# A fused layer on one core: the first stage's queues reordered, the rounding constant taken off on ScalarE, masked CB in PSUM, chains interleaved

## The chip, the cores and the metric

One core of a Trainium2 chip runs the whole program. The metric is the device time of one execution in microseconds (us). The engines are named as in the profile: PE is TensorE, DVE is VectorE, ACT is ScalarE, POOL is GpSimd, SP issues DMAs. Each has its own queue and works it off in order; semaphores order them against each other. SBUF is the large on-chip memory, PSUM the one that PE writes.

## What is computed

8192 tokens (64 sequences of 128) pass through an embedding, a state-space layer (SSD) and a mixture of experts. All in float32:

```python
scale = jnp.maximum(jnp.max(jnp.abs(weight), axis=-1, keepdims=True) / 127, 1e-8)
h = (jnp.clip(jnp.round(weight / scale), -127, 127) * scale)[input]       # rows of 192

zxbcdt = layernorm(h) @ in_proj_w.T                  # z 384, xBC 384 + 2 * 128, dt 6
dt = softplus(zxbcdt[..., -6:] + dt_bias)
xBC = silu(sum(conv_w[:, k] * xp[:, k:k + L, :] for k in range(4)) + conv_b)
CB = einsum('bcln,bcsn->bcls', C, B)                 # one chunk of 128 a sequence
Y = einsum('bcls,bhcls,bcshp->bclhp', CB, exp(segsum(dt * A)), x * dt) + D * x
y = Y * silu(z);  y = y * rsqrt(mean(y * y) + eps) * norm_w
h = h + sigmoid(gate1) * (y @ out_proj_w.T) + layernorm(h)

h2 = layernorm(h)                                    # route_c, route_u: argmax of two softmaxes of 4
common = expert(route_c)(h2)                         # gelu(x @ W1 + b1) @ W2 + b2, 192 -> 768 -> 192
dropped = rank within route_c (by confidence) >= 2048
out = h + common + dropped * expert(route_u)(h2)
```

## The kernel before

The program has two stages. The first is a software pipeline over 16 groups of four sequences. In turn `t`, `body(t, g1, g2, g3, g4, g5)` works on five groups at once: the embedding and first norm of group `t` and `t + 1`, the projection and convolution of group `t - 1` (`g2`), the SSD of `t - 2` (`g3`), output product, residual and second norm of `t - 3` (`g4`), and the routing of `t - 4` (`g5`). Turns 0 to 17 make the stage. The second stage runs expert units of 256 tokens (gather, two products, scatter), with a search for the capacity threshold beside it; the diff leaves it alone but for the places where it calls functions of the first.

The order of the work within a turn is written out by hand, once for each engine (`body` in each of the blocks `tensor`, `scalar`, `vector`, `gpsimd`). Since queues are worked off in order, a wait holds everything behind it.

The steps that matter, with their lines:

- `project(m)` (PE, L1131): tile m of the projection, 5 of xBC (m < 5), 3 of z. The part over the last 64 channels is issued for two tiles at once in the odd m (L1151), so both become ready then. Only two banks, `mm0` and `mm1`, hold them: `project(m)` waits until tile m - 2 has been read.
- `start(m)` (ACT, L795): first tap and bias out of PSUM into `xbc` (m < 5); z tiles by copy or Silu. `conv(m)` (DVE, L1518): the three other taps, each reading PSUM and `xbc` and waiting for the one before. `silus` (ACT): Silu over all of `xbc`, then over the first z tile.
- `cbx(j)` (PE, L1077): for sequence j, C·B and the transposes of x into the bank `cx`. `seg(j)` (PE, L1057): the differences of running sums into banks `sg0` and `sg1`, which `decays(j)` (ACT, L784) empties by Exp into `dec`. `weights(j)` (DVE, L1533): `cbm` = CB times the causal mask, `xd` = x times dt, and `mix` = min(dec, 1) times `cbm`, six heads of 128. `y(j)` (PE): the product of the two, then `y(j)` (DVE, L1549) adds D·x, and `gate_y(j)` (POOL, L541) multiplies by Silu of z.
- `softplus` (DVE, L1488): ten small operations, each waiting for the one before, that give dt and at the end `drep`; `step_sums` (PE) and `sum_rows` (ACT, L823) turn these into the rows `rows_s` that `seg` of the next turn reads.
- `squares` (ACT), `side` (PE, L1100), `copy_side` (ACT), `side_back` (PE), `side_read` (DVE, L1469): sums of squares, dt and routing values of a group, collected by small products, transposed and read once.
- `quantise(g)` (DVE, L1420) finds the scale of gathered rows; `rounded(g)` (ACT, L773) multiplies and adds 12582912, which rounds; `clip(g)` (DVE, L1431) subtracts that constant and clips, in two passes of 128x768, and takes the statistics. `norm1`, `normed`, `with_rest`, `to_tp`, `from_tp` bring the normed rows to the transposed tiles that `project` reads.
- `residual`, `stats2`, `logits`, `pick`, `places` (DVE), `prefixes` (PE), `list_tokens` (POOL): second residual and norm, routing, running counts `acc` and `more` for each expert, and the lists of tokens. Routing goes in batches of two groups, so that `logits` and `pick` stand in every second turn, `places`, `prefixes` and `list_tokens` in the others.

A `Chain` counts operations of one engine that need each other: `link(ins)` issues one and waits until it has finished; `link.go(ins)` issues only, and `link.join()` waits later.

## Time and profile before

| | us |
|---|---|
| median of 3 runs | 1097.21 (1094.24 to 1099.18) |
| profiled execution | 1107.01 |
| its span, first to last instruction | 1105.2 |
| busy, share of the span: PE | 84% |
| DVE | 61% |
| ACT | 51% |
| POOL | 52% |
| mean granted TensorE clock | 0.925 of 2.4 GHz |

The page gives shares over the whole span; the 40 slices of its second part show which engine is full when. Below that the trace can be asked for windows (busy time by stretch), for groups of instructions by line, and for timelines, in which a bracket names the idle time ahead of an instruction and what ended it. "issue" in it is idle time for which the profile shows no releaser. PEclk is the granted clock as a share of full speed.

### The profile page before, as it was taken

Reading aid. Unit: us, or ns where it says so; the run is one execution under the profiler, and the core shown is the slowest. Engines: PE = TensorE matmul, PEld = TensorE weight load, DVE = VectorE, ACT = ScalarE, POOL = GpSimd, SP = SyncE. Lnnn points to the kernel's source line nnn. Section 1 sums busy time; section 2 is a strip of 40 time slices with the busy share of each in tenths; the row PEclk is TensorE's granted clock in tenths of the full one; section 3 lists DMA queues with packets and bytes.
Section 4 is the critical chain, followed back from the end, with each engine's and each line's share of the span. In section 5 each row is a group of like instructions: output and inputs, shape, how many; then the busy total and the mean of one; then the engine's idle time right before and its main releaser. Section 6 shows DMA issues by size and latency. Waiting matters only on the chain.

```text
span 1105.2 us, 18876 instructions
## 1 busy us (share of the span) xinstructions
PE 931.3 (84%) x5730; PEld 626.5 (57%) x5731; DVE 679.1 (61%) x2089; ACT 564.6 (51%) x1163; POOL 573.0 (52%) x751
## 2 busy tenths in 40 slices
PE   2688899888888889989888597999897977979986
PEld 2233455445554555545546475767675756768874
DVE  3687999898998989889887234777211211112111
ACT  3666886777767877588664224232232221323330
POOL 7332645456465655463434555234556656556543
PEclk9898998999999998899997788999888979889988
DMA  4910011001110111010001122133332111112211
GB/s 101 319 50 2 15 44 45 30 17 45 44 42 6 44 45 45 2 45 30 30 31 60 34 64 66 58 99 111 90 89 54 54 46 49 49 54 73 73 56 29
DMA packets 50179, 61.91 MB, mean 56 GB/s; under 512 B 22668, under 2 KB 41832, under 8 KB 49556
## 3 DMA queue, kind: packets, MB, share of 16 engines
q0 software_dynamic: 16704, 30.54, 9.8%
q1 hardware_dynamic: 28724, 24.91, 7.6%
q10 hardware_dynamic: 4640, 5.13, 1.5%
q8 instruction: 51, 0.84, 0.3%
q14 instruction: 60, 0.49, 0.1%
HBM read 36.22 MB, written 25.92 MB: 56 GB/s over the span
## 4 chain that ended last, share of the span: by engine, by line
PE 40%; DVE 24%; issue 13%; ACT 12%; another core or an unknown queue 5%; POOL 3%; DMA 2%; DVEq 1%; ACTq 0%; POOLq 0%
DVE xbc L1526 9%; PE yb L1304 5%; PE mm L1147 5%; PE cx L1304 5%; PE mm L1282 4%; PE mm L1275 4%; PE mm L1151 3%; PE sg L1275 3%; DVE mix L1546 2%; PE tp L1114 2%; PE sg L1065 2%; ACT rows_s L831 2%; DVE ybuf L1559 2%; DMA xg<-hr_dram,ids 1%
## 5 line engine op out<-in xcount | busy, mean ns | idle before, releaser
L1526 DVE SCALAR_TENSOR_TENSOR xbc<-mm,cw,xbc 128x508 f32<-128x508 f32 (+2 forms) x231 | 168.5, 741 | 27.5 <-ACT xbc L806 19.9
L1147 PE MATMUL mm<-xt_a,win_a 128*128 128x512 f32 x248 | 144.2, 666 | 38.0 <-DVE xbc L1526 28.8
L979 ACT ACTIVATE ht<-mm,b1s 128x256 f32<-128x256 f32 x102 | 44.8, 473 | 256.8 <-PE sg L1275 119.9
L689 POOL DMA_INDIRECT out_dram<-osb,ids_s x80 | 81.9, 1024 | 139.4 <-DVE osb L1900 122.9
L1900 DVE TENSOR_TENSOR osb<-cx,res 128x192 f32<-128x192 f32 x40 | 14.3, 357 | 180.0 <-remote 90.3
L806 ACT ACTIVATE xbc<-mm,cb,cw 128x512 f32<-128x512 f32 x77 | 56.5, 774 | 123.2 <-PE mm L1151 122.2
L549 POOL TENSOR_TENSOR ybuf<-ybuf,zs 128x384 f32<-128x384 f32 x64 | 69.3, 1084 | 73.7 <-DVE ybuf L1559 71.6
L670 POOL DMA_INDIRECT xg<-hr_dram,ids x80 | 80.4, 1005 | 47.6 <-issue 23.8
L1304 PE MATMUL yb<-w2s,ht 128*128 x408 | 85.1, 359 | 10.3 <-issue 10.2
L1304 PE MATMUL cx<-w2s,ht 128*128 x408 | 77.8, 337 | 14.9 <-issue 14.9
L1275 PE MATMUL mm<-fx_a,w1a_t 128*128 128x256 f32 x240 | 82.1, 426 | 9.6 <-issue 5.7
L1304 PEld LDWEIGHTS yb<-w2s,ht 128*128 128x128 f32 x408 | 75.6, 210 | 18.2 <-issue 17.9
L1147 PEld LDWEIGHTS mm<-xt_a,win_a 128*128 128x128 f32 x248 | 39.3, 199 | 76.1 <-DVE xbc L1526 47.2
L1065 PE MATMUL sg<-rows_s,rows_t 32*128 32x384 f32 x256 | 62.8, 568 | 18.9 <-ACT rows_s L831 17.5
L1546 DVE SCALAR_TENSOR_TENSOR mix<-dec,cbm 128x768 f32<-128x768 f32 x64 | 72.0, 1125 | 10.5 <-ACT dec L791 10.5
L608 POOL DMA_INDIRECT list_c<-tok,desti x64 | 64.6, 1010 | 26.2 <-issue 18.1
L1282 PE MATMUL mm<-fx_b,w1b_t 64*128 64x256 f32 x240 | 77.3, 431 | 0.0
L1282 PE MATMUL sg<-fx_b,w1b_t 64*128 64x256 f32 x240 | 77.3, 431 | 0.0
L1304 PEld LDWEIGHTS cx<-w2s,ht 128*128 128x128 f32 x408 | 68.2, 196 | 13.8 <-issue 13.5
L1275 PE MATMUL sg<-fx_a,w1a_t 128*128 128x256 f32 x240 | 74.9, 395 | 0.0
L1151 PE MATMUL mm<-xt_b,win_b 64*128 64x512 f32 x248 | 74.5, 679 | 0.0
L517 POOL DMA_INDIRECT gath<-in_table_dram,gidx x64 | 63.9, 998 | 19.6 <-issue 14.9
(304 smaller groups left out, 2101.1 us busy)
## 6 DMA issues: line engine op xcount, KB each, us to landing
hr_dram<-hr SPq DMA_DIRECT2D x16, 768.0 KB
w2s<-in_w2c_dram SPq DMA_DIRECT2D x4, 576.0 KB
w2s_u<-in_w2u_dram ACTq DMA_DIRECT2D x4, 576.0 KB
list_c<-fill SPq DMA_DIRECT2D x2, 1032.0 KB, 12.4
list_u<-fill SPq DMA_DIRECT2D x2, 1032.0 KB, 18.7
w1a<-in_w1c_dram SPq DMA_DIRECT2D x4, 384.0 KB
w1a_u<-in_w1u_dram ACTq DMA_DIRECT2D x4, 384.0 KB
xg<-hr_dram,ids POOLq DMA_INDIRECT x80
```

The source lines that it names most:

```text
L549: nc.gpsimd.tensor_tensor(ybuf[:, p, :, js], ybuf[:, p, :, js], zs[:, p, :, js], ALU.mult).then_inc(s_y2, 1)
L608: nc.gpsimd.indirect_dma_start(out=list_c[:, :], out_offset=bass.IndirectOffsetOnAxis(ap=desti[:, p, j:j + 1], axis=0), in_=tok[:, GS * fi ...
L670: nc.gpsimd.indirect_dma_start(out=xg[:, v, t, :], out_offset=None, in_=rows, in_offset=bass.IndirectOffsetOnAxis(ap=ids[:, v, t, 0:1], ax ...
L689: nc.gpsimd.indirect_dma_start(out=out_rows, out_offset=bass.IndirectOffsetOnAxis(ap=ids_s[:, v, t, 0:1], axis=0), in_=osb[:, v, t, :], in ...
L1065: last = mmul(bank_[:, 0:HPB * P], rows_t[r:r + ROWS, :], rows_s[r:r + ROWS, j // 2, :, :], start=True, stop=True)
L1147: mmul(tile_bank(g2, m)[:, :], win_a[:, column(m):column(m) + P], xt_a[:, p, :], start=True, stop=False)
L1151: mmul(tile_bank(g2, m - 1 + n)[:, :], win_b[r, c0:c0 + P], xt_b[r, p, :], start=False, stop=True).then_inc(s_mm, 1)
L1275: last = mmul(hid[n][c // 2][:, c % 2 * TL:(c % 2 + 1) * TL], w1a_t[:, v, (3 * n + c) * P:(3 * n + c + 1) * P], fx_a[:, :], start=first, s ...
L1282: last = mmul(hid[n][c // 2][:, c % 2 * TL:(c % 2 + 1) * TL], w1b_t[r, v, c * P:(c + 1) * P], fx_b[r, :], start=first, stop=not first)
L1304: last = mmul(outp[t][:, 0:D], ht[:, v, k, t * P:(t + 1) * P], w2_[:, ds(e * (FC * D) + k * D, D)], start=(k == 0), stop=(k == FC - 1))
L1526: ins = stt(out=dst_[:, :, back:L], in0=src[:, :, 0:L - back], scalar=cw[:, m, TAPS - 1 - back:TAPS - back], in1=dst_[:, :, back:L], op0=A ...
L1546: stt(out=mix[:, j % 2, :, :], in0=dec[:, j % 2, :, :], scalar=1.0, in1=cbm[:, :].unsqueeze(1).broadcast_to([P, HEADS, P]), op0=ALU.min, o ...
```

## The change

Orders first. DVE takes `logits` and `conv(0)` ahead of `weights(0)`; `weights(j)` is cut into `scaled(j)` (mask and x·dt) and `mixed(j)`, which stand apart with other work between; `quantise` goes behind `side_read`. ACT takes `start(0)` ahead of `decays(0)`, `decays(3)`, `with_rest`, `from_tp(0)` ahead of `start(4)`, and the rounding ahead of the Silus. PE takes both first projections ahead of `cbx(0)`, `side` ahead of `y(1)`, `to_tp(0)` ahead of `project(5)`, and `step_sums` last. In `clip` the subtraction goes to ACT as a fifth pass. The masked CB is written back into its PSUM bank, so `cbx(j + 1)` waits for `mix` j. The steps of softplus, of pick and of the second statistics are issued between other operations. The running count lies in the same tile as the one-hots (`oh` has two more rows, used from either end in turn), and one reduction adds it up. The gathers take their index straight from `xids`.

```diff
-STEPS = dict(norm=5, quant=2, clip=3, ...)
+STEPS = dict(norm=5, quant=2, clip=2, ...)
@@ gpsimd
-                nc.gpsimd.tensor_copy(gidx[:, p, :], xids[:, GS * g:GS * (g + 1)]).then_inc(s_idx, 1)
-                pool.wait_ge(s_idx, g + 1)
...
-                        in_offset=bass.IndirectOffsetOnAxis(ap=gidx[:, p, j:j + 1], axis=0)).then_inc(s_gath[p], 16)
+                        in_offset=bass.IndirectOffsetOnAxis(ap=xids[:, GS * g + j:GS * g + j + 1], axis=0)).then_inc(s_gath[p], 16)
@@ scalar, rounded
-                last.then_inc(s_rd, 1)
+                last.then_inc(s_whole, 1)
+                act.wait_ge(s_whole, g + 1)
+                nc.scalar.activation(h0[:, :, :], h0[:, :, :], ACT.Identity, bias=magic[:, 1:2], scale=1.0).then_inc(s_rd, 1)
@@ scalar, order of a turn
+                start(0)
                 decays(0)
-                start(0)
                 start(1)
                 decays(1)
                 normed2()
                 squares()
-
+                exp_logits()
                 start(2)
                 start(3)
                 decays(2)
                 normed()
                 copy_side()
-
-                start(4)
-                exp_steps()
-                start(5)
-                exp_logits()
+                decays(3)
                 with_rest()
                 from_tp(0)
-                decays(3)
-                silus()
+                exp_steps()
+                start(4)
+                start(5)
                 if t + 1 < NG:
                     rounded(t + 1)
+                silu_z()
+                silu_xbc()
                 from_tp(1)
                 start(6)
                 start(7)
@@ tensor, cbx
-                    wait(pe, s_xd, GS * g3 + j)
+                    wait(pe, s_m, GS * g3 + j)
@@ tensor, order of a turn
                 project(0)
+                project(1)
                 cbx(0)
+                prefixes()
                 seg(0)
-                project(1)
                 seg(1)
-                prefixes()
+                project(2)
+                cbx(1)
                 y(0)
-                cbx(1)
-
-                project(2)
+                seg(2)
                 project(3)
-                seg(2)
+                side()
                 y(1)
-                side()
-
+                seg(3)
+                cbx(2)
                 project(4)
-                cbx(2)
+                to_tp(0)
                 side_back()
                 project(5)
                 out_product(0)
-                to_tp(0)
-                seg(3)
+                to_tp(1)
+                cbx(3)
                 y(2)
-
                 project(6)
-                cbx(3)
                 out_product(1)
-                to_tp(1)
-                step_sums()
                 project(7)
                 y(3)
+                step_sums()
@@ vector
-                link(ts(h0[:, :, :], h0[:, :, :], MAGIC, QMAX, ALU.subtract, ALU.min))
-                link(ts(h0[:, :, :], h0[:, :, :], -QMAX, None, ALU.max))
+                link(ts(h0[:, :, :], h0[:, :, :], QMAX, -QMAX, ALU.min, ALU.max))
...
-                        if back < TAPS - 1:
-                            link(ins)
+                            link.go(ins)
+                            beside[back - 1]()
+                            link.join()
...
-                    link(tt(cbm[:, :], cx[:, 0:P], le[:, :], ALU.mult))
+                    link.go(tt(cx[:, 0:P], cx[:, 0:P], le[:, :], ALU.mult))
...
+                def mixed(j):
+                    chains["ssd"].join()
                     dve.wait_ge(s_e, GS * g3 + j + 1)
                     stt(out=mix[:, j % 2, :, :], in0=dec[:, j % 2, :, :], scalar=1.0,
-                        in1=cbm[:, :].unsqueeze(1).broadcast_to([P, HEADS, P]), op0=ALU.min, op1=ALU.mult).then_inc(s_m, 1)
+                        in1=cx[:, 0:P].unsqueeze(1).broadcast_to([P, HEADS, P]), op0=ALU.min, op1=ALU.mult).then_inc(s_m, 1)
...
-                    v.tensor_reduce(more[:, :], oh[:, 0:n5, 0, :].rearrange("p j e -> p e j"), AX.X, ALU.add).then_inc(s_oh, 1)
...
-                    tt(acc[:, :], acc[:, :], more[:, :], ALU.add)
+                    v.tensor_reduce(running(b + 1), with_running(b, n), AX.X, ALU.add)
@@ vector, new order of a turn (all of it)
+                logits(); conv(0); weights(0); conv(1); y(0)
+                scaled(1); places(); mixed(1); conv(2); conv(3)
+                scaled(2); y(1); side_read(); steps_abs(); quantise(t + 1); mixed(2)
+                conv(4, (soft_sum, soft_inverse)); soft_ratio()
+                residual(0, (0,)); soft_square(); residual(0, (1,)); soft_top()
+                scaled(3); soft_term(3); mixed(3); soft_term(2); soft_term(1); soft_term(0); soft_steps()
+                y(2); residual(1); soft_rates(); rows_read()
+                pick((row_moments 0 to 3, row_sums, row_shift))
+                y(3); clip(t + 1)
@@ vector, old order of a turn (all of it)
-                weights(0); conv(0); conv(1); y(0); places()
-                weights(1); conv(2); conv(3); y(1)
-                quantise(t + 1); side_read(); steps_abs(); logits()
-                weights(2); conv(4); residual(0); softplus(); y(2)
-                weights(3); residual(1); pick(); stats2(); y(3); clip(t + 1)
```

(The two orders of DVE's turn are set on fewer lines here than in the code.)

## Rows read from the trace of the kernel before

**Rows 1.** The page: busy tenths of DVE in 40 slices of the span.

```profile
DVE  3687999898998989889887234777211211112111
```

**Rows 2.** Windows: us, busy us (x) PE, PEld, DVE, ACT, POOL, PEclk, DMA.

```profile
127.49:552.86 425.37, 376.32 (x2678) 216.39 (x2676) 385.44 (x1077) 317.39 (x588) 231.31 (x351) 0.97 0.11 33
...
321.63:357.06 35.43, 31.34 (x228) 17.82 (x225) 30.44 (x83) 27.04 (x50) 21.03 (x31) 1.00 0.12 35
357.06:392.59 35.53, 29.88 (x225) 17.54 (x223) 34.07 (x100) 26.36 (x49) 20.87 (x31) 1.00 0.11 35
...
428.77:466.60 37.83, 34.92 (x229) 21.43 (x228) 34.30 (x100) 26.95 (x50) 20.89 (x31) 0.86 0.11 34
...
611.40:1105.20 493.80, 416.64 (x2216) 333.25 (x2214) 157.93 (x641) 137.87 (x372) 258.35 (x264) 0.89 0.23 64
```

**Rows 3.** Timeline of DVE, turn starts: start, us, instruction, [idle before <-releaser].

```profile
340.49 0.26 DVE L1540 TENSOR_TENSOR cbm<-cx,le 128x128 f32<-128x128 f32 x1
...
342.52 0.96 DVE L1546 SCALAR_TENSOR_TENSOR mix<-dec,cbm 128x768 f32<-128x768 f32 x1 [1.18 <-ACT dec L791]
344.29 4.50 DVE L1526 SCALAR_TENSOR_TENSOR xbc<-mm,cw,xbc 128x508 f32<-128x508 f32 x6 [0.81 <-ACT xbc L806]
...
377.66 0.26 DVE L1540 TENSOR_TENSOR cbm<-cx,le 128x128 f32<-128x128 f32 x1
...
411.44 0.26 DVE L1540 TENSOR_TENSOR cbm<-cx,le 128x128 f32<-128x128 f32 x1
```

**Rows 4.** Timeline of DVE: the two clip passes.

```profile
375.01 0.55 DVE L1434 TENSOR_SCALAR h<-h 128x768 f32<-128x768 f32 x1
375.60 0.56 DVE L1435 TENSOR_SCALAR h<-h 128x768 f32<-128x768 f32 x1
```

**Rows 5.** DVE by line, 127.49:552.86: xcount | busy us, mean ns | idle before.

```profile
L1546 DVE SCALAR_TENSOR_TENSOR mix<-dec,cbm 128x768 f32<-128x768 f32 x48 | 54.7, 1139 | 5.0 <-ACT dec L791 5.0
...
L1637 DVE TENSOR_TENSOR acc<-acc,more 128x4 f32<-128x4 f32 x6 | 5.0, 836 | 0.2
```

**Rows 6.** Line 1526, the taps: xcount, ns min/median/max, first and last start.

```profile
L1526 DVE SCALAR_TENSOR_TENSOR xbc<-mm,cw,xbc x231: 732/740/749, 33.5 to 575.4; 128x508 f32<-128x508 f32 x39, 128x500 f32<-128x500 f32 x39, 128x504 f32<-128x504 f32 x38
```

**Rows 7.** Timelines of POOL and DVE: gate product, mix beside it.

```profile
359.71 1.00 POOL L549 TENSOR_TENSOR ybuf<-ybuf,zs 128x384 f32<-128x384 f32 x1
...
360.05 1.48 DVE L1546 SCALAR_TENSOR_TENSOR mix<-dec,cbm 128x768 f32<-128x768 f32 x1
```

**Rows 8.** Timeline of DVE in pick: two that wait, two that don't.

```profile
371.33 0.22 DVE L1613 TENSOR_REDUCE m<-pk 128x16 f32<-128x64 f32 x1
371.59 0.22 DVE L1614 TENSOR_TENSOR oh<-pk,m 128x64 f32<-128x64 f32 x1
...
372.34 0.17 DVE L1618 COPY ohc<-oh 128x32 f32<-128x32 f32 x1
372.42 0.17 DVE L1619 COPY ohu<-oh 128x32 f32<-128x32 f32 x1
```

**Rows 9.** ACT by line, 127:553: start(m) and the rounding passes.

```profile
L806 ACT ACTIVATE xbc<-mm,cb,cw 128x512 f32<-128x512 f32 x60 | 44.0, 774 | 93.8 <-PE mm L1151 92.8 <-issue 1.0
...
L778 ACT ACTIVATE h<-gath,magic,q 128x192 f32<-128x192 f32 x44 | 20.3, 533 | 0.0
```

**Rows 10.** Timeline of ACT: table load ahead of the first decays.

```profile
340.32 1.28 ACT L791 ACT_TABLE_LOAD   x1
```

**Rows 11.** Timeline of PE: gap in side, seg, projection, slow seg.

```profile
320.87 0.88 PE L1114 MATMUL tp<-ybuf,wy 128*32 128x128 f32 x20 [1.00 <-issue]
...
340.36 0.91 PE L1065 MATMUL sg<-rows_s,rows_t 32*128 32x384 f32 x4 [1.19 <-ACT rows_s L831]
...
342.25 1.13 PE L1151 MATMUL mm<-xt_b,win_b 64*128 64x512 f32 x4
...
449.13 1.65 PE L1065 MATMUL sg<-rows_s,rows_t 32*128 32x384 f32 x4
```

**Rows 12.** Timeline of POOL: gate product behind the list transfers.

```profile
345.60 1.00 POOL L549 TENSOR_TENSOR ybuf<-ybuf,zs 128x384 f32<-128x384 f32 x1
```

More of the change, by code:

```diff
@@ L192, in build @@
         ohu = sb("ohu", [P, SEQS, NE])
-        acc, more = sb("acc", [P, NE]), sb("more", [P, NE])
         w1a = sb("w1a", [P, NE * F])
@@ L721, in _ @@
             norm2()
+            route()
             gather_unit(0, 1, 1, 1)
@@ L1194, in prefixes @@
                     wait(pe, s_h1, 2 * cap(t - 3 if t <= LAST_SSD else t - 2))
+                    oh_, acc = picked(b, n)[:, :, 0, :], running(b)
                     if b == BATCHES - 1:
@@ L1516, in softplus, with nothing, conv @@
                     last.then_inc(s_dt, 1)
-                def conv(m):
+                def nothing():
+                    pass
+                def conv(m, beside=(nothing, nothing)):
                     if g2 is None:
@@ L1585, in stats2, with rows_read, row_moments, row_sums @@
                                chains["h1"]).then_inc(s_ve2, 1)
+                    chains["h1"].end()
+                def rows_read():
+                    if g4 is not None:
+                        dve.wait_ge(s_h1, 2 * g4 + 2)
+                        wait(dve, s_xn2, g4)
+                def row_moments(j):
+                    if g4 is not None:
+                        ins = v.bn_stats(st2[:, j, :], hr[:, g4 % 2, j, 0:D])
+                        if j == GS - 1:
+                            chains["h1"].go(ins)
+                def row_sums():
+                    if g4 is None:
+                        return
+                    chains["h1"].join()
+                    for j in range(GS):
+                        last = v.bn_aggr(mv2[:, j, :], st2[:, j, :])
+                    chains["h1"].go(last)
+                def row_shift():
+                    if g4 is None:
+                        return
+                    chains["h1"].join()
+                    ts(var2[:, :], mv2[:, :, 1], LNEPS, None, ALU.add)
+                    ts(minus2[:, :], mv2[:, :, 0], -1.0, None, ALU.mult).then_inc(s_ve2, 1)
                     chains["h1"].end()
@@ L1599, in logits, with pick @@
                     link.end()
-                def pick():
+                def pick(beside=(nothing,) * 6):
                     if b5 is None:
+                        for other in beside:
+                            other()
                         return
```

207 lines of the change are left out of this document (135 added, 72 removed).

## The prediction

> **What bounds the kernel now.** I read the page first. In its 40 slices the Vector engine (DVE) stands at nine tenths in most slices from the third to the twenty-first, and then drops to one or two, while PE stays high to the end: two stages, and the change touches only the first [rows 1]. The windows by stretch give sizes. From 127.49 to 552.86 us, twelve turns of 35.45 us, DVE is busy for 385.44 of 425.37 us, PE for 376.32, ACT for 317.39, POOL for 231.31. After 611.40 come 493.8 us in which DVE is busy for 158: the expert units, which no edit reaches [rows 2].
>
> Third, DVE's timeline. Turns alternate. One with logits and pick (the L turn, 340.49 to 377.66) takes 37.17 us, one with places (the P turn, to 411.44) 33.79: a pair is 70.95. The L turn has 2.0 us of waits at its start: `mix` waits 1.18 for ACT's decays, the first tap 0.81 for ACT's first copy out of PSUM [rows 3]. Three more waits of 0.5 to 0.65 stand in the pair, so DVE works for about 67.2 us of 70.95. DVE sets the pace, PE is close behind: its busy time at full clock is 31.34 and 29.88 us in the two windows of one pair, 30.6 a turn [rows 2].
>
> **The change part by part: DVE.** All sums are for a pair.
>
> The clip pass that subtracts the rounding constant starts 0.59 us ahead of the next one: 2 x 0.59 = 1.2 us removed [rows 4].
>
> `mix`: 48 of them take 1139 ns on average, an undisturbed one 0.96 [rows 3, 5]. The excess comes when POOL runs a tensor operation: its gate product starts at 359.71 and takes 1.00, `mix` starts at 360.05 and takes 1.48 [rows 7]. The masked CB in PSUM leaves `mix` one SBUF tensor. No such `mix` is in this trace. The nearest rows are the taps, one tensor in PSUM and one in SBUF: 231 of them lie between 732 and 749 ns, so POOL never stretched one [rows 6]. Bounds: nothing gained (even 0.06 us lost each, if PSUM reads are dearer) to 0.19 us each. I take 0.19, as the taps are alike in kind: 8 x 0.19 = 1.5.
>
> The running count `acc` plus `more` takes 836 ns for 4 elements, beside the same POOL product, plus 0.12 for `more` [rows 5]. One reduction with one input replaces both, 0.2 us: 0.7 saved.
>
> Interleaved chains: an operation that waits for the one before it starts 0.26 us after it (371.33 to 371.59), one that doesn't starts 0.08 us after it (372.34 to 372.42) [rows 8]. With the larger operand of the chain counted, a hidden wait is worth about 0.12 us. Six in pick (L turn only), six of softplus and two in the last channel's taps each turn, one behind each of the eight CB maskings: 6 + 16 + 8 = 30 waits, 3.6 us; I take 3.2, as some of the filling operations wait themselves. The Trainium skill (VectorE: DVE Perf Modes, The DRAIN you can't avoid) says that eight copies take the same time with a semaphore after each as with one behind the last. By it these 3.2 us would be nothing; these rows disagree for small operations.
>
> DVE's work falls by 1.2 + 1.5 + 0.7 + 3.2 = 6.6 us, from 67.2 to 60.6: 30.3 a turn. That is below PE's 30.6, so what is late next is PE.
>
> **ACT.** It takes the constant off instead: one pass over 128x768. The 192-wide form takes 533 ns, the 512-wide one 774, so 0.75 ns an element: an estimate of 0.97 us, and it must wait for the four passes before it, 0.1 more [rows 9]. ACT goes from 26.4 to 27.5 us a turn, idle before it being mostly the waits for projections (93.8 us over the twelve turns, before copies out of PSUM) [rows 9]. Behind that wait stand both Silus, `from_tp(1)` and the last two z tiles, which release PE's next project(0). Its bounds are 0.8 and 1.3 us. With no cover it costs 1.1 us a turn.
>
> **The order.** I lay the new queues out with these durations (PE: projection pair 3.06 us, seg 0.86 [rows 11]; CB and transposes 0.71, y 0.8, side 2.2, out product 2.0, prefixes 2.1, by the starts on PE's timeline; all of PE's pieces sum to 30.4 a turn, against 30.6 in [rows 2]). Zero is PE's project(0). Project(1) ends at 3.06, ACT's start(0) lets conv(0) begin at 4.05. seg(0) ends at 4.6. Here is a new wait: ACT's table load of 1.28 us stands before the first decay, now behind start(0), and seg(1) needs the banks that decays(0) empties [rows 10]. So seg(1) starts at 6.1, and PE, in order, holds project(2), cbx(1) and y(0) behind it; 1.5 us idle. In P turns prefixes fill it, but then it all comes 1.6 us later. DVE has conv(0) as cover meanwhile, so the 2.0 us at the start of a turn go. Then conv(1) ends at 10.0, project(3) at 12.4, and conv(2) begins at 13.3 after 1.0 us of wait; side ends at 14.6, side_back at 18.6; conv(3) ends at 17.7, project(5) at 20.7. start(4), moved behind `with_rest` and `from_tp(0)`, is on ACT at 20.8. ACT then runs start(5), the rounding with its new pass, the table load, Silu of z and of xBC, from_tp(1), start(6): to 30.4. PE reaches y(3) and the step sums at 30.8, DVE its last clip at 34.85, which is 4.05 of the next turn. All three engines close the turn within 0.5 us of each other: 30.8 us for L, and by the same steps 32.5 for P, 31.7 on average.
>
> The new wait of cbx(j+1) for `mix` j instead of `xd` j costs nothing while a scaled and mixed pair lies two convs ahead of its cbx. In the last turn of the stage (from 592 us) there are no taps: there it puts about 0.9 us in each of two or three places: 1.5 to 2 us lost. Gather's direct index saves POOL 0.5 us a turn, off the path; rounding reached earlier helps the gathers.
>
> Layouts by hand have no gaps. The trace has: PE stands still for 1.00 us within side with nothing to wait for [rows 11], about once a turn. So I add 1.0: 32.7 a turn instead of 35.45. Over twelve turns 33 us; the three outer turns, with DVE less full, 2 each: 6; less 1.5 for the last: 37.5. Clock: at the lower level seg takes 1.65 instead of 0.91 us [rows 11], and the window at 0.86 holds 34.92 us of PE work [rows 2]. Three such stretches lie in the stage; DVE's pace covered most of them, and will no longer. The forecast takes nothing for them beyond the 1.0, nor for small gains in turns 0 and 1.
>
> Against the profiled execution, 1107.0 us of which 1105.2 are span: 1069.5. The median of the runs is 1097.2, 9.8 lower; 3.4% of it is 37.5, so 1059.7; I say 1059.
>
> **Rivals.**
>
> A, bubbles take half of it. PE queue waits in order: if what I count as 1.0 us of gaps and 1.5 at seg(1) is double, because side now stands ahead of y(1), seg(3), cbx(2) and project(4) and itself waits for ACT's squares (which are done at 11.0 against 12.4 needed), a turn takes 34.2. For it: PE and ACT slack of under 1 us everywhere in the layout; in the P turn POOL's gate_y(3) comes after four list transfers [rows 12] and only 0.8 us before squares need it. Against: ACT waits 8 us a turn for projections now, room to slip. Saving 1.25 x 12 + 3: 1097 - 18 = 1079.
>
> B, the Vector engine keeps its work: the chains give nothing (the skill's rule above) and `mix` is as long as now in PSUM. Then only 1.9 of 6.6 go, DVE works 32.65 a turn, about 33.6 with a wait of 1: saving 1.85 x 12 + 5 = 27, 1070. Against it stand [rows 6, 8]. The rule of the skill alone (3.2 of 6.6 gone) would leave DVE 31.9 a turn, 33.2 with its waits, and give about 1065; of B's chance 0.02 is for it.
>
> C, slower: TensorE's clock. DVE hid it before; now PE's work is the turn. In the stretch at 0.86 PE worked 34.92 us in 37.83. With the 2.0 us of waits of the new order such a turn is 36.9. If the whole first stage ran so, it would be 1.45 x 15 = 22 us slower: 1119. It decides from a granted mean of about 0.9 in that stage, 0.97 now. For it: the drops are there, and came in turns whose rows before them look like those of turns without one (the 1.19 us of wait for `rows_s` is in each) [rows 11]. Against: PE gets fuller, not emptier, and in the first stage most windows are at 1.00.
>
> **How the numbers follow.** The forecast, 1059, with its own range 1042 to 1070 (all gaps gone: 31.7 a turn and 49 us saved, 1048, and 6 for the outer turns; `mix` or ACT's pass at the bad end): 0.55. A, 1079: 0.25. B, 1070: 0.10. C, 1119: 0.04. The rest, 0.06, is spread, a third of it slower. The range runs from 1040 to 1086. A measurement of this kernel tells about 0.5% from no change, 5.5 us. Faster by more: 0.88. Within: 0.06. Slower by more: 0.06.
>
> **What would show it.** In the new profile: first stage shorter by about 38 us, the second alike; DVE busy near 30 us a turn and no longer the fullest, PE above it; every `mix` near 0.95 to 1.0 us; the count's reduction near 0.2; small operations 0.1 apart; one ACT pass of about 1 us; PE idle before seg(1), by ACT `dec`, of 1 to 1.5 us; no wait of the first conv on `dec`. Wrong if `mix` still varies with POOL, if ACT's rounding is what releases the clip or project(0) late, if PE waits for ACT's squares in side, or if the granted clock of the first stage falls below 0.9.

## The result, and the profile after

Beside each other, 20 runs each: before 1098.16 us (1091.07 to 1105.71), after 1089.78 us (1080.29 to 1097.51). The ratio is 0.9909, 95% interval 0.9882 to 0.9937: faster by 8.4 us, where 38 were forecast, and outside the range. The profiled execution took 1090.97 us, 1089.2 of them span. The one of before took 1107.01, some 9 above its median, so the two profiles lie 16 us apart where the medians lie 8.4.

The page of after, DVE and the granted clock in 40 slices of the span, and the engines' shares of the chain that ended last; below them the windows (us, busy us (x) PE, PEld, DVE, ACT, POOL, PEclk, DMA) of the first and second stage:

```profile
DVE  3668898979988889788787136787121112112220
...
PEclk9889999999998889888988788999898988989998
...
PE 66%; issue 12%; DVE 8%; ACT 6%; another core or an unknown queue 4%; POOL 2%; DMA 1%; DVEq 1%; POOLq 0%; ACTq 0%
```

```profile
127.00:548.00 421.00, 392.56 (x2685) 225.52 (x2686) 361.36 (x1062) 333.32 (x604) 214.97 (x344) 0.93 0.11 34
598.20:1089.00 490.80, 414.79 (x2219) 328.87 (x2217) 158.00 (x641) 138.66 (x372) 259.33 (x264) 0.91 0.23 65
```

Against [rows 1, 2], DVE has fallen from 385 to 361 us in a window of about twelve turns, and PE has risen from 376 to 393: PE is now the fullest engine, at a granted clock of 0.93 instead of 0.97. The first expert unit starts at 598.2 instead of 610.7. So in these two profiles the first stage is 12.5 us shorter, not 38, and the second nearly alike (491 us for 494). The twelve turns average 34.9 us (418.4 over 12) against a forecast of 32.7. Here and below a turn runs from one masking of sequence 0's CB on DVE to the next.

The pieces on DVE and ACT came as forecast. Timeline of DVE (a masking, xd, `mix`, a tap; the count's reduction) and of ACT (the new pass), and line 1595, the `mix` of that window, with ns min/median/max:

```profile
262.83 0.29 DVE L1584 TENSOR_TENSOR cx<-cx,le 128x128 f32<-128x128 f32 x1
263.02 0.55 DVE L1586 TENSOR_TENSOR xd<-cx,dts 128x384 f32<-128x384 f32 x1
263.49 0.94 DVE L1595 SCALAR_TENSOR_TENSOR mix<-dec,cx 128x768 f32<-128x768 f32 x1
264.35 0.74 DVE L1570 SCALAR_TENSOR_TENSOR xbc<-mm,cw,xbc 128x508 f32<-128x508 f32 x1
...
302.07 0.22 DVE L1735 TENSOR_REDUCE oh<-oh 128x4 f32<-128x36 f32 x1
```

```profile
280.34 0.94 ACT L794 ACTIVATE h<-h,magic 128x768 f32<-128x768 f32 x1
```

```profile
L1595 DVE SCALAR_TENSOR_TENSOR mix<-dec,cx x49: 935/945/955, 128.0 to 546.4; 128x768 f32<-128x768 f32 x49
```

There is no wait between the `xd` at 263.02, the `mix` and the tap: the 2.0 us of [rows 3] are gone. What is new stands on PE. Its timeline in one L turn, ACT's beside it, and windows of 2 us over the same stretch (PEclk is the third number from the end):

```profile
327.99 0.92 PE L1084 MATMUL sg<-rows_s,rows_t 32*128 32x384 f32 x4
330.51 1.65 PE L1084 MATMUL sg<-rows_s,rows_t 32*128 32x384 f32 x4 [1.61 <-ACT dec L805]
332.10 2.08 PE L1166 MATMUL mm<-xt_a,win_a 128*128 128x512 f32 x2
```

```profile
328.20 1.28 ACT L805 ACT_TABLE_LOAD   x1
329.50 0.87 ACT L805 ACTIVATE dec<-sg 128x384 f32<-128x384 f32 x2
```

```profile
328.00:330.00 2.00, 0.91 (x5) 0.29 (x4) 1.93 (x8) 1.97 (x4) 1.38 (x2) 1.00 0.01 2
330.00:332.00 2.00, 1.49 (x4) 0.53 (x4) 1.97 (x5) 1.04 (x2) 1.62 (x2) 0.62 0.03 6
332.00:334.00 2.00, 2.00 (x5) 0.88 (x4) 1.93 (x4) 1.80 (x5) 1.75 (x2) 0.50 0.09 16
334.00:336.00 2.00, 2.00 (x14) 1.67 (x14) 0.51 (x1) 2.00 (x3) 1.75 (x6) 0.50 0.02 4
336.00:338.00 2.00, 2.00 (x13) 1.02 (x10) 1.17 (x5) 0.33 (x2) 1.84 (x5) 0.67 0.00 0
```

seg(1) waits 1.61 us for decays(0), which stand behind the table load, as laid out. But then the granted clock goes from 1.00 to 0.50, that is from 2.4 to 1.2 GHz, and stays there for almost 7 us. seg(1) takes 1.65 us instead of 0.92. Such a stretch stands near the start of all seven turns from 330 us on; most turns before them have none or one of half that length. From 30 to 620 us the time at 1.2 GHz ("low clock" below) sums to 105 us; in the trace of before to 60.

And in P turns side is longer than before. PE's timeline, products of four with nothing to wait for:

```profile
305.40 0.42 PE L1133 MATMUL tp<-ybuf,wy 128*32 128x128 f32 x4 [0.30 <-issue]
306.12 0.43 PE L1133 MATMUL tp<-ybuf,wy 128*32 128x128 f32 x4 [0.30 <-issue]
306.85 0.42 PE L1133 MATMUL tp<-ybuf,wy 128*32 128x128 f32 x3 [0.31 <-issue]
307.58 0.27 PE L1133 MATMUL tp<-ybuf,wy 128*32 128x128 f32 x1 [0.30 <-issue]
308.30 0.28 PE L1133 MATMUL tp<-ybuf,wy 128*32 128x128 f32 x1 [0.45 <-issue]
```

Undisturbed, side takes 2.23 us (in L turns, in both traces). In P turns it took up to 4.4 before and takes 4.9 to 5.8 now (3.3 in the first).

### The profile page after: what moved, and what is told of

Same layout as the page of the kernel before. It is cut to its first block, busy times and chain, and to the rows that moved or that the text cites. A ratio compares the mean times of both kernels' runs of the same rounds, so it can differ in the third digit from the quotient of the medians.

```text
span 1089.2 us, 18793 instructions
## 1 busy us (share of the span) xinstructions
PE 942.1 (86%) x5730; PEld 630.2 (58%) x5731; DVE 643.2 (59%) x2064; ACT 584.1 (54%) x1179; POOL 548.2 (50%) x736
## 4 chain that ended last, share of the span: by engine, by line
PE 66%; issue 12%; DVE 8%; ACT 6%; another core or an unknown queue 4%; POOL 2%; DMA 1%; DVEq 1%; POOLq 0%; ACTq 0%
PE mm L1166 11%; PE mm L1170 6%; PE misc L1181 5%; PE yb L1321 5%; PE sg L1084 5%; PE cx L1321 5%; PE yb L1115 5%; PE mm L1299 4%; PE mm L1292 4%; PE tp L1133 3%; PE sg L1292 3%; PE cx L1105 2%; PE cx L1103 2%; DVE xbc L1570 2%
## 5 line engine op out<-in xcount | busy, mean ns | idle before, releaser
L559 POOL TENSOR_TENSOR ybuf<-ybuf,zs 128x384 f32<-128x384 f32 x64 | 64.2, 1003 | 111.9 <-DVE ybuf L1613 109.9
L1084 PE MATMUL sg<-rows_s,rows_t 32*128 32x384 f32 x256 | 67.9, 608 | 24.9 <-ACT dec L805 22.9
L1321 PEld LDWEIGHTS yb<-w2s,ht 128*128 128x128 f32 x408 | 73.1, 204 | 24.9 <-issue 24.4
L1181 PEld LDWEIGHTS misc<-wo,ybuf 128*128 128x128 f32 x384 | 63.7, 194 | 20.7 <-issue 19.5
L805 ACT ACTIVATE dec<-sg 128x384 f32<-128x384 f32 x128 | 55.7, 490 | 35.5 <-PE sg L1084 34.2
L527 POOL DMA_INDIRECT gath<-in_table_dram,xids x64 | 63.2, 988 | 19.4 <-issue 17.0
L1181 PE MATMUL misc<-wo,ybuf 128*128 128x192 f32 x384 | 71.4, 337 | 1.5 <-DVE sd L1494 1.4
L660 POOL DMA_INDIRECT list_u<-tok,slot_u x64 | 62.9, 982 | 19.5 <-issue 19.5
```

What stands on the lines that cost most here:

```text
L527: nc.gpsimd.indirect_dma_start(out=gath[:, p, j, :], out_offset=None, in_=A["table"][:, :], in_offset=bass.IndirectOffsetOnAxis(ap=xids[:, ...
L559: nc.gpsimd.tensor_tensor(ybuf[:, p, :, js], ybuf[:, p, :, js], zs[:, p, :, js], ALU.mult).then_inc(s_y2, 1)
L1084: last = mmul(bank_[:, 0:HPB * P], rows_t[r:r + ROWS, :], rows_s[r:r + ROWS, j // 2, :, :], start=True, stop=True)
L1181: last = mmul(misc[:, OUTC + j * D:OUTC + (j + 1) * D], ybuf[:, g4 % 2, c, (2 * q + j) * L:(2 * q + j + 1) * L], wo[:, c, :], start=(c == ...
L1321: last = mmul(outp[t][:, 0:D], ht[:, v, k, t * P:(t + 1) * P], w2_[:, ds(e * (FC * D) + k * D, D)], start=(k == 0), stop=(k == FC - 1))
```

## The experiments

All start from the changed kernel unless said. The kernel before took about 1030 us beside some kernels and about 1100 beside others, on the same chips (last section), so all comparisons are by the ratio to the kernel before in the same batch; that level is given with each. Rows with the same level were run together; between rows of different levels a small difference says less than its interval. Only the change and spare_product were run at both levels. "Units" is the start of the first expert unit, and "low" the time at 1.2 GHz from 30 to 620 us, both in the profiled execution (before: 610.7 and 60).

| kernel | level | ratio, 95% interval | units, us | low, us |
|---|---|---|---|---|
| lists_late | 1031 | 0.9965, 0.9938 to 0.9992 | 595.6 | 119 |
| seg_first | 1031 | 0.9816, 0.9777 to 0.9855 | 590.2 | 130 |
| spare_product | 1031 | 0.9651, 0.9620 to 0.9681 | 565.7 | 61 |
| work_only | 1031 | 1.0123, 1.0093 to 1.0153 | 611.2 | 77 |
| the change again | 1099 | 0.9895, 0.9845 to 0.9945 | 595.7 | 99 |
| orders_only | 1099 | 0.9996, 0.9964 to 1.0028 | 610.7 | 109 |
| spare_elsewhere | 1099 | 0.9967, 0.9934 to 1.0000 | 603.3 | 92 |
| seg_first_spare | 1099 | 0.9755, 0.9710 to 0.9800 | 580.9 | 65 |
| spare_again | 1106 | 0.9791, 0.9746 to 0.9836 | 582.6 | 59 |
| spare_lists_late | 1106 | 0.9718, 0.9681 to 0.9756 | 576.8 | 55 |
| linked | 1106 | 1.0035, 1.0008 to 1.0063 | 614.7 | 51 |
| mask_sbuf | 1106 | 0.9584, 0.9550 to 0.9618 | 563.3 | 54 |
| mask_sbuf_no_spare | 1030 | 0.9863, 0.9818 to 0.9908 | 590.3 | 102 |
| seg_first_mask | 1030 | 0.9615, 0.9584 to 0.9647 | 559.2 | 48 |
| clip_on_dve | 1030 | 0.9691, 0.9663 to 0.9719 | 572.0 | 75 |
| lists_end | 1030 | 0.9666, 0.9632 to 0.9699 | 567.6 | 48 |
| seg_first_mask again | 1028 | 0.9609, 0.9575 to 0.9642 | 559.2 | 45 |
| the change once more | 1028 | 0.9852, 0.9821 to 0.9883 | 585.1 | 102 |

### Does PE's wait at seg(1) cost the clock?

In PE's turn, one product that nothing reads, where PE waits (spare_product, spare_again) or later, behind seg(2), where it doesn't (spare_elsewhere):

```
 seg(0)
+mmul(tp[:, :], ident[:, :], xt_a[:, g2 % 2, :], start=True, stop=True)   # spare_product
 seg(1)
 project(2); cbx(1); y(0)
 seg(2)
+mmul(...the same...)                                                      # spare_elsewhere
```

> The changed kernel with one product more in each turn on PE, between seg(0) and seg(1): a 128x512 product into the transposing bank that nothing reads, about 1.0 us, in the place of the wait for decays(0). Theory 3, the low level of the clock in every later turn (6.8 us at 1.2 GHz from the turn's start) comes from the emptiness there: low time in the first stage falls from 105 us to about 60 as before, mean clock of 127 to 548 us from 0.93 to 0.97, and the time by 10 to 20 us to 1070 to 1080, though PE has 16 us of work more. Otherwise: low time as it was, and the time 1090 to 1096.

> As spare_product, with the same unread 128x512 product into tp, but behind seg(2), where TensorE has no idle time, instead of ahead of seg(1). Theory 1 (the product helped since it filled the idle time ahead of seg(1)): low stretches as in the changed kernel, 100 to 120 us; ratio as the changed kernel's or up to 0.3% above it (0.43 us of product a turn). Theory 2 (any more work on TensorE, or the shift of tp, would have done it): as spare_product, ratio 0.965, 61 us of low clock.

> The changed kernel itself, on the same chip as the experiments. Theory 1 (the wait of seg(1) behind the decays brings TensorE's clock down, wherever it runs): granted clock of stage 1 about 0.92 to 0.93, low stretches of 6.8 us in most turns, 100 to 130 us of low clock in all, ratio to the kernel before 0.99 to 1.00 (lists_late, nearly the same kernel, gave 0.9965). Theory 2 (what was lost on the first chip is the gaps of 0.30 us inside side's products, beside the list transfers): without such gaps on this chip the ratio is 0.97 to 0.975, and the low stretches are no more than the 60 us of the kernel before.

> The changed kernel beside it. On the faster chip, where it has not been run: theory 1 (the gaps in side are only on the other chip, the clock is lost on both): side 2.23 in P turns, 100 to 120 us of low clock, ratio 0.990 to 0.998, since lists_late, nearly the same kernel, gave 0.9965 there. Theory 2 (lists_late was itself worse than the changed kernel where there are no gaps): 0.975 to 0.988. On the slower chip: 0.99 as twice before.

The same added work gives 0.9651 (level 1031) and 0.9791 (1106) ahead of seg(1), and 0.9967 behind seg(2); the change itself has 0.9852 (1028), 0.9895 and 0.9909 (about 1099). Windows of spare_product, spare_elsewhere and the change once more; how long the seg products waited in the change and in spare_product (line, x, busy us, mean ns, idle before); and the added product in an L turn, with the seg(1) behind it:

```profile
127.00:548.00 421.00, 408.14 (x2913) 234.37 (x2911) 384.47 (x1158) 352.54 (x635) 222.19 (x351) 0.96 0.11 36
```

```profile
127.00:548.00 421.00, 395.49 (x2704) 227.28 (x2704) 358.38 (x1058) 332.58 (x601) 212.73 (x340) 0.94 0.11 34
```

```profile
127.00:548.00 421.00, 398.82 (x2803) 230.45 (x2803) 370.06 (x1080) 341.07 (x618) 217.25 (x345) 0.92 0.11 34
```

```profile
L1084 PE MATMUL sg<-rows_s,rows_t 32*128 32x384 f32 x196 | 52.5, 614 | 17.6 <-ACT dec L805 17.6
```

```profile
L1084 PE MATMUL sg<-rows_s,rows_t 32*128 32x384 f32 x208 | 51.5, 572 | 6.5 <-ACT dec L805 4.4 <-ACT rows_s L851 2.1
```

```profile
314.07 1.12 PE L1092 MATMUL tp<-xt_a,ident 128*128 128x512 f32 x2
315.75 0.91 PE L1084 MATMUL sg<-rows_s,rows_t 32*128 32x384 f32 x4 [0.55 <-ACT dec L805]
```

The product takes 1.1 us at full clock (the expectation of spare_elsewhere has 0.43, which is too little) and fits into the wait of 1.6. With the idle time filled, the waits of the seg products fall from 17.6 us (in both traces of the change) to 6.5, low clock from 102 to 61 us, and the first expert unit starts at 565.7 instead of 585.1. The same product later leaves 92 us of low clock, against 99 in its batch, and makes the kernel no faster than the change but some 0.7% slower, with intervals that meet. So it is the idle time at that place, not added work or its tile. Each pair below is from two batches of nearly one level: the product is worth 0.020 (0.9852 to 0.9651, 21 us) where side has no gaps, and 0.010 (0.9895 to 0.9791, 11 us, give or take 7 by the two intervals) where it has. At the upper level P turns were to be 33 to 34 us with a ratio of at most 0.978; the later ones are 34.2 to 34.8 at full clock, and the ratio just misses it. The change once more has the ratio of its theory 2 and the low clock and the short side of its theory 1: lists_late was 1.1% worse than the change, so the "0.9965" on which two expectations rested was a poor stand-in.

The Trainium skill (TensorE: Matmul & The Clock Gate, A second HAM failure mode: psum-queue depth-cycling) tells of a kernel whose TensorE idles briefly between groups of products and swings between the two clocks. The windows of the change agree: a wait of 1.61 us in a thin stretch, 0.50 behind it.

Moving seg(0) instead, ahead of cbx(0) and the prefixes, so that these fill the wait in P turns; alone (seg_first), and with the spare product in L turns (seg_first_spare):

```
 project(1)
+seg(0)
 cbx(0)
 prefixes()
-seg(0)
+if listed_turn(t)[0] is None: spare_product()     # seg_first_spare only
 seg(1)
```

> The changed kernel with PE's seg(0) ahead of cbx(0) and prefixes. If the wait of seg(1) for decays(0) (1.61 us in L turns, 1.06 in P turns) is on the path: cbx (0.7 us) and prefixes (2 us) fill it, the wait falls to about 0.9 in L turns and to 0 in P turns, a pair gains 1.8 us, about 12 us in all: 1078. If PE waits later by the same amount for DVE or ACT: within 4 of 1090. If the wait also brings the clock down, the 6.8 us at 1.2 GHz at turn starts become fewer and it gains up to 20.

> seg(0) ahead of cbx(0) and the prefixes, so that cbx(0) and in P turns the prefixes lie between seg(0) and seg(1), and the unread 128x512 product between them only in L turns, where there are no prefixes. Theory 1 (only idle time ahead of seg(1) counts): both kinds of turn are filled, low clock 60 us or less, ratio 0.960 to 0.966. Theory 2 (seg(0) itself is late in this order, as in seg_first, whose turns were all 34.1 us with a low stretch in each): low clock 100 to 130 us, ratio 0.975 to 0.985.

seg_first has more low clock than the change (130 us, some 6.8 in nearly every turn), and its turns are nearly all of 33.9 to 34.5 us; its ratio is that of the change once more, within the intervals. (Its profiled execution took 1021.8 us, 7 above its median, so its low clock may be on the high side.) That the order gained in P turns about what the clock lost there fits these numbers, but isn't shown. With the spare product in L turns low clock is 65 us, and the ratio 1.4% below that of the change in its batch. The clock does respond to the filled place again. But the ratio of 0.9755 is above my 0.960 to 0.966, and side takes 4.4 to 5.6 us in its P turns: the second loss.

### The gaps in side

list_tokens(0), four indirect transfers, in POOL's turn from ahead of `rms` to behind `gate_y(1)`: in the change (lists_late) and in spare_product (spare_lists_late).

```
 gate_y(0)
-list_tokens(0)
 rms()
 gate_y(1)
+list_tokens(0)
```

> The changed kernel with one move on POOL: the first four list transfers of a turn go behind rms and gate_y(1). The result is the same. In the changed kernel side takes 5.5 us on PE in P turns and 2.2 in L turns; the gaps in it (0.30 us ahead of every four products, no releaser) lie beside these transfers. Theory 1, the transfers of POOL slow the supply of PE's instructions: side falls to 2.2 to 2.5 us in P turns, a pair of turns at full clock falls from 67.9 to about 65 us, and the time to about 1070 (1090 less 20). Theory 2, PE's queue has no lead left after the many small products of prefixes: side stays at 5.5 us and the time at 1090 within 4.

> The kernel of spare_product once more, as the base of the three kernels beside it, and to see it on the chip where side's products have gaps of 0.30 us if it lands there. Theory 1 (the clock was the larger part of the loss and the gaps the smaller): low clock about 60 us, 31.6 us a turn at full clock after an L turn; where the gaps of 0.30 us show, P turns are 33 to 34 and the ratio 0.970 to 0.978; where they don't, 0.965. Theory 2 (the gaps were the larger part): where they show, the ratio is that of the changed kernel, 0.99.

> As spare_product, with the first half of the list transfers behind the rms and gate_y(1) of GpSimd, so that it is issued some 5 us later, behind side. Theory 1 (the gaps of 0.30 us every four products of side come while list transfers are issued and land): side takes 2.2 to 2.9 us in P turns also where it took 4.5 to 5.6; there the ratio is 0.5 to 1% below spare_again's. Theory 2 (the gaps belong to the short products of side, TensorE's queue running empty behind the prefixes, whatever GpSimd issues): side as long as in spare_again, the same ratio or up to 0.3% more. Where spare_again has no gaps, the two theories give the same, 0.965.

lists_late fell on the 1031 level, where neither it nor any other kernel had a gap in side; it tells nothing of them, only that the later lists seem to cost 1.1% against the change of another batch. spare_again and spare_lists_late are a pair in one batch. PE's timeline, the end of side in the same P turn, first spare_again, then spare_lists_late:

```profile
299.75 0.42 PE L1139 MATMUL tp<-ybuf,wy 128*32 128x128 f32 x4 [0.32 <-issue]
300.51 0.41 PE L1139 MATMUL tp<-ybuf,wy 128*32 128x128 f32 x3 [0.35 <-issue]
301.27 0.42 PE L1139 MATMUL tp<-ybuf,wy 128*32 128x128 f32 x4 [0.35 <-issue]
302.71 0.38 PE L1139 MATMUL tp<-ybuf,wy 128*32 128x128 f32 x2 [1.02 <-issue]
```

```profile
296.20 0.86 PE L1139 MATMUL tp<-ysq,wq 128*32 128x128 f32 x24
296.88 0.84 PE L1139 MATMUL tp<-ybuf,wy 128*32 128x128 f32 x24
297.65 0.55 PE L1121 MATMUL yb<-mix,xd 128*64 128x128 f32 x6
```

Side falls from 5.80 to 2.23 us here, and is 2.23 in all P turns. The ratio falls by 0.007, with intervals that just meet, and not by the 0.016 that the 18 us of gaps in the six P turns would be; a new wait opens elsewhere. DVE's timeline in spare_lists_late: POOL issues eight transfers in a row until 314.73, and the residual of the second half stands for 2.92 us although PE's output product ended at 311.0 (14.0 us in the twelve turns, none in spare_again; what releases it the profile doesn't name):

```profile
314.88 0.42 DVE L1637 SCALAR_TENSOR_TENSOR hr<-misc,rs,hx 128x192 f32<-128x192 f32 x1 [2.92 <-remote]
```

All lists at the end of POOL's turn, from a base without gaps:

> As seg_first_mask, with all list transfers of a P turn at the end of GpSimd's turn, behind gate_y(3), some 20 us behind side. Theory 1 (the gaps of 0.30 us in side are caused by list transfers in flight, whichever kernel): side takes 2.23 in every P turn, also where seg_first_mask has it longer; ratio as mask_sbuf's 0.958 or, against a seg_first_mask with gaps, 0.015 below it. Theory 2 (the gaps depend on how a kernel's instructions lie in memory, not on the transfers): side keeps 4.4 or more in some P turns; ratio as seg_first_mask's.

No gaps in it or in its base: it tells only that lists at the end cost 0.5%, within the intervals. What is shown: in one pair the gaps go when the transfers go. Not shown: why they come only at the 1100 level, and not in every P turn there. In mask_sbuf the first P turn has them and the next five don't, though the first list transfer is issued 0.3 us ahead of side as in spare_again; in orders_only, also with the mask in SBUF, three P turns have them and three don't. From mask_sbuf's timeline, side in the first P turn, then in the third:

```profile
164.67 0.43 PE L1140 MATMUL tp<-ybuf,wy 128*32 128x128 f32 x4 [0.32 <-issue]
...
292.84 0.84 PE L1140 MATMUL tp<-ybuf,wy 128*32 128x128 f32 x24
```

So transfers in flight are not enough for a gap. Its cause stays open.

### Orders and work apart

> The changed kernel with the orders of the kernel before on DVE, ACT and PE (weights ahead of conv(0), decays ahead of start(0), rounding behind the Silus, side behind y(1), and so on); the work cuts stay: one clip pass on ACT, masked CB in PSUM, one reduction for the count, interleaved chains. My prediction had DVE at 60.6 us a pair by these cuts and put 2.0 us a pair on the order. If the cuts carry the gain: 1090 to 1093. If the order carries it: 1096 to 1100, with DVE idle where it worked before. If the order costs, through side and seg(1): below 1088.

> The orders of the change on all three engines, with the work of the kernel before (clip in two VectorE passes, the mask to SBUF, linked small operations, acc and more). Theory 1 (the orders carry the gain where the clock stays up, the work removed is worth little by itself): VectorE keeps some 33.6 us a turn, so turns of 34 to 35; the wait of seg(1) is in the orders, so the low stretches come too (80 to 130 us); ratio 0.995 to 1.01. Theory 2 (the work removed from VectorE was the gain, the orders are neutral): ratio 1.00, no more low clock than in the kernel before (60 us). Theory 3 (orders alone hold the whole gain): 0.985 or less.

work_only keeps every cut of work and the old orders on PE, ACT and DVE: `body()` of the three engines has the order of before. orders_only is the opposite: clip in two passes, the mask to `cbm`, each chain linked, `acc` and `more`, with the orders of after. Neither is faster than before; work_only is 1.2% slower than before, where I expected at most 0.2%. There, `mix` waits for ACT's decays 26.9 us in 421, against 5.0 in [rows 5]:

```profile
L1598 DVE SCALAR_TENSOR_TENSOR mix<-dec,cx 128x768 f32<-128x768 f32 x48 | 45.4, 945 | 26.9 <-ACT dec L805 26.9
```

The work removed from DVE became a longer wait for ACT in the old order. That ACT's new pass is what delays those decays was not tried. orders_only is as its theory 1 had it: 109 us of low clock, so the new orders bring the clock's loss by themselves. Against the change in its batch (0.9996 and 0.9895) the work cuts are worth 0.010 in the new orders.

### The prices of single edits

On spare_product, the waits of the chains put back behind each operation (linked), and the mask to SBUF (mask_sbuf, where cbx still waits for `mix`):

```
-class Chain: go() issues, join() waits later
+class Eager(Chain): go(ins) waits at once

-link.go(tt(cx[:, 0:P], cx[:, 0:P], le, ALU.mult)) ; mix reads cx
+link.go(tt(cbm, cx[:, 0:P], le, ALU.mult))        ; mix reads cbm
```

> As spare_product, but each small VectorE operation of the chains waits for the one before it at once, with the other chain's work not between them (Eager instead of Chain; softplus, pick and statistics as issued, each with its wait behind it). Theory 1 (a dependent small operation costs 0.24 to 0.26 us and an independent one 0.12, so the interleaving was worth 1.6 to 1.8 us a turn, and VectorE is at its bound at 31.6): VectorE's load rises by 1.5 us a turn, the ratio by 0.010 to 0.018 above spare_again's. Theory 2 (the waits that the interleaving removes cost nothing, since VectorE drains between any two operations): VectorE as loaded, ratio within 0.003 of spare_again's.

> As spare_product, but the masked CB is written to SBUF (cbm) as in the kernel before, with mix reading it from there. Theory 1 (mix is slowed by GpSimd's traffic only when both its inputs are in SBUF): the mean of mix goes from 0.95 back to 1.05 to 1.15 us, VectorE's load up by 0.4 to 0.8 us a turn, ratio 0.004 to 0.009 above spare_again's. Theory 2 (mix was long for another reason, and the changed orders alone took GpSimd's traffic away from it): mean 0.95 to 1.0, ratio within 0.002.

linked is 0.024 above spare_again, 27 us over 16 turns, 1.7 us a turn: theory 1, over its range. By pairs of turns at full clock it is more, 71.0 us against 66.4. The rule of the Trainium skill (VectorE: DVE Perf Modes, The DRAIN you can't avoid), by which the waits cost nothing, does not hold for these small operations.

mask_sbuf surprised: 0.021 below spare_again where I expected 0.004 to 0.009 above. Line 1604 of mask_sbuf and 1602 of spare_again, then mask_sbuf's windows:

```profile
L1604 DVE SCALAR_TENSOR_TENSOR mix<-dec,cbm x53: 939/949/1401, 129.5 to 546.5; 128x768 f32<-128x768 f32 x53
```

```profile
L1602 DVE SCALAR_TENSOR_TENSOR mix<-dec,cx x51: 935/944/955, 126.4 to 543.3; 128x768 f32<-128x768 f32 x51
```

```profile
127.00:548.00 421.00, 404.12 (x2935) 233.06 (x2931) 390.67 (x1165) 352.89 (x636) 240.26 (x353) 0.99 0.12 37
```

In SBUF a `mix` can still be stretched (to 1401 ns), in PSUM none is. But the means are 981 and 945 ns, 0.15 us a turn: under the new orders POOL's gate product rarely meets a `mix`. That is why mask_sbuf loses little; what it gains is elsewhere. Five of its P turns have side at 2.23 us, 16 us less in all than in spare_again. Three of spare_again's P turns have 6.8 us of low clock, and none of mask_sbuf's in that stretch. And where neither has gaps or low clock its pairs take 64.5 us against 63.5 in spare_product: 0.5 us a turn lost by the mask in SBUF, the size of theory 1 but not its mechanism, as `mix` has only 0.15 of it. Gaps and clock together cover that loss and more. Why the gaps stay away is open, as said, and so is whether the clock stayed up for want of gaps.

From seg_first_spare with the mask in SBUF, the kernel with the lowest times; with the clip's subtraction back on DVE; and the change with only the mask in SBUF:

> seg_first_spare (seg(0) ahead of cbx(0), spare product only in L turns) with the masked CB in SBUF. The base of the two kernels beside it. Theory 1 (the mask in PSUM is worth about what mix gains, 0.0 to 0.5 us a turn, and mask_sbuf's gain over spare_again is the absence of gaps in side): ratio 0.955 to 0.962 if side takes 2.2 in P turns, 0.970 to 0.980 if it takes 4.4 to 5.6. Theory 2 (the mask in PSUM costs 1 to 2 us a turn by itself, through cbx): 0.955 to 0.962 in both cases.

> The kernel of seg_first_mask once more. On the faster chip (the kernel before at about 1030 us) it should give 0.960 again, with no gap in side. On the other (about 1100 us): theory 1 (the gaps of 0.30 us in side come with list transfers in flight, for any kernel on that chip): side 4.4 to 5.7 in P turns, ratio 0.972 to 0.978, as seg_first_spare (0.9755). Theory 2 (the gaps go by how the kernel's code or buffers lie, as mask_sbuf without them at the same lead suggests, and the mask's place changed that): side 2.23, ratio 0.955 to 0.960, as mask_sbuf (0.9584).

> As seg_first_mask, with the rounding constant subtracted by VectorE again (two passes over 128x768, no pass on ScalarE). Theory 1 (VectorE is at its bound at 32 us a turn, so each pass of 0.57 us counts in full): VectorE's load up by 0.6 us a turn, ratio 0.005 to 0.007 above seg_first_mask's. Theory 2 (ScalarE's pass of 0.95 us delays what TensorE waits for, and the pass back on VectorE lies in its idle time): ratio the same or up to 0.5% below. Both within what five rounds can just tell.

> The changed kernel with the one edit of mask_sbuf (masked CB in SBUF) and without the spare product. On mask_sbuf itself TensorE stayed at full clock from 85 to 538 us, so this takes the spare product away where nothing else is amiss. Theory 1 (the wait of seg(1) for the decays brings the clock down in most turns, whatever else): low clock 100 to 120 us against 54 in mask_sbuf, most of it as 3.4 or 6.8 us behind seg(1), ratio 0.978 to 0.988 (mask_sbuf: 0.958). Theory 2 (the mask in PSUM holds the bank that cbx needs, and that was what made TensorE idle and the clock fall): low clock stays at 55 to 70, ratio 0.955 to 0.963. Theory 3 (neither: mask_sbuf was short only since the gaps in side were absent): low clock as theory 1, side 2.2 in P turns where mask_sbuf had it so.

seg_first_mask gives 0.9615 and 0.9609; 988 us against 1028 before and 1014 of the change: 2.5% under the change. Both times it fell on the level without gaps. As neither run has gaps, they decide between none of their theories. clip_on_dve is 0.0076 above its base, 7.8 us over 16 turns, 0.49 a turn: theory 1, though low clock is 75 us there against 48, so part of it may be the clock. Its L turns at full clock take 32.4 us against 31.8, so the pass counts in full there. mask_sbuf_no_spare falls back to 0.9863 and 102 us of low clock, so the spare product is what holds the clock with the mask in SBUF too, though mask_sbuf itself was run at the other level; at this level the change has 0.9852, so here the mask's place is worth nothing that the runs can tell.

## Why the prediction was wrong

The frame held: DVE set the pace, PE was next, the change reached only the first stage. So did most steps.

- Clip, 1.2 a pair: right (clip_on_dve: 0.49 a turn against 0.6).
- `mix`, 1.5 a pair: right in size (1139 to 946 ns), and the cause is one of two that each suffice. With the mask in PSUM and the old orders (work_only) the mean is 945; with the mask in SBUF and the new orders (orders_only) it is 955. The Trainium skill (GPSIMD Engine Reference, Key points) names GpSimd's contention with VectorE operations in a 2-port perf mode or with two SBUF inputs; the maxima agree for the second kind, 1787 ns before in SBUF, 955 in PSUM.
- Count, 0.7: right (0.22 us). Chains, 3.2: right or too low (linked: 3.4 a pair by the times, 4.5 by the turns at full clock). ACT's pass: 0.94 for 0.97.
- DVE 30.3 us a turn: measured 361.36 in 421 us, 30.0 per turn of 34.9. I had missed one contention: quantise's small `q<-q` now meets the gate product and takes 1012 ns instead of 170, beside it as `mix` was in [rows 7]. From the timelines of POOL and DVE:

```profile
277.18 1.00 POOL L559 TENSOR_TENSOR ybuf<-ybuf,zs 128x384 f32<-128x384 f32 x1
...
277.19 1.00 DVE L1443 TENSOR_SCALAR q<-q 128x4 f32<-128x4 f32 x1
```

- The order, 31.7 a turn: right if the clock stays up and side has no gaps. At full clock spare_product takes 31.6 us for L and at most 31.9 for P turns. The halves were off against each other: laid out were 30.8 and 32.5.
- The gaps, 1.0 a turn: mis-sized a little. They stand in P turns alone, where side is 2.7 to 3.5 us too long from the second on, 17 us in the twelve turns; before it was 10. Not all of that is turn time: at full clock a P turn with 3.6 us of gaps takes 34.8 (spare_again), one without 31.9 (spare_product). So they cost 14 to 17 us where I charged 12.
- Clock: the step that failed. "The forecast takes nothing for them", and C, "PE gets fuller, not emptier", had 0.04. I had laid out the 1.5 us wait of seg(1) myself, and priced it as 1.5 us. It also brings the clock down for almost 7 us. A low L turn takes 34.6 instead of 31.6. The spare product, which keeps part of these stretches away, gave back 11 us at this level and 21 at the other.

The account of the 26 us missing over twelve turns (34.9 less 32.7, 2.2 a turn): the order at full clock nothing (31.75 for 31.7), the gaps 0.2 to 0.4 beyond what was charged, and the rest, 1.7 to 2.0 a turn or 21 to 24 us, the clock. That last term is a difference, not a measurement; three us for each low L turn agree with it. Where the clock mostly stays up and there are no gaps, spare_product is 3.5% under before, as much as the forecast of 3.4%. Of the rivals, A named the outcome in size (34.2 a turn, 1079) with another mechanism: side did not wait for the squares. C named the mechanism, but I tied it to a whole stage below 0.9; it was 0.93, with most turns paying part of it. B's two parts both fell. The range ended at 1086, 4 us short of the median. At the other level the change is 1.5% under before, still less than half of what I forecast.

## What to carry to other kernels

Price a short wait on TensorE in a thin stretch by what the clock does after it, not by its own length: look whether every turn will have it, and fill it. Here an unread product did it; useful work that can be moved there would be better, but the one move tried, seg_first, did not hold the clock. When the work and the order of a loop change together, neither need be worth anything alone. And charge gaps seen in one kind of turn to that kind of turn, with the transfers that lie beside them.

## What the runs showed that was not expected

- One unread product of 1.1 us in the place of a wait made the kernel 1 to 2% faster.
- The same kernel took about 1030 us in some batches and about 1100 in others; two of the three chips showed both. The first stage of the change is nearly alike (598.2, 595.7, 585.1 us); its second takes 491 us at a clock of 0.91, or 429 at 0.96. At the 1100 level the products of the expert units are preceded by `issue` gaps that the other level lacks. Line 1321 of the page of after, two groups (x, busy us, mean ns, idle before):

```profile
L1321 PE MATMUL yb<-w2s,ht 128*128 x408 | 84.6, 352 | 17.1 <-issue 17.0
...
L1321 PEld LDWEIGHTS yb<-w2s,ht 128*128 128x128 f32 x408 | 73.1, 204 | 24.9 <-issue 24.4
```

These look like the gaps in side. What sets the level of a batch isn't known.
- The gaps in side went when GpSimd's indirect transfers were moved away, but two other kernels lack them in part of their P turns with the transfers in place.
